# A four-layer graph network on one core: 0/1 matrices on GpSimd and results kept in PSUM late in layer 0, own products earlier in the attention layer

## What is computed

```python
edge_index = jnp.stack([src, dst])                     # 25000 edges, sorted by dst
x = _layernorm(x + _L0_gnn_ref(x, Wq, Wk, Wv, src, dst))
x = _layernorm(x + _L1_gnn_ref(x, edge_index, ...))
x = _layernorm(x + _L2_gnn_ref(x, edge_index, ...))
x = _layernorm(x + _L3_gnn_ref(x, edge_index, edge_attr, ...))

# layer 0: attention without a maximum; 8 heads of 32
score = jnp.exp(jnp.clip(sum(k[src] * q[dst]) / sqrt(32), -5.0, 5.0))
out = segment_sum(v[src] * score, dst) / (segment_sum(score, dst) + 1e-09)

# layer 2: graph attention with a loop at every node
e = leaky(a_src[src] + a_dst[dst])                     # loops included
alpha = softmax of e over the edges of one dst
y = segment_sum(h[src] * alpha, dst) + bias + x
return layernorm(y) * ln_w + ln_b
```

## Time and profile before

| | |
|---|---|
| median of 3 runs | 4683.01 us (4680.12 to 4685.71) |
| profiled execution | 4724.27 us |
| its span | 4722.6 us, mean granted clock 0.948 |
| busy share of the span | PE 93%, DVE 84%, POOL 66%, ACT 56% |
| `layer0` | about 30 to 1052 us |
| `nodes1` | about 1052 to 2466 us |
| `nodes2` | about 2466 to 3490 us |
| `layer3` | about 3490 to 4722 us |

### The profile page before, as it was taken

The page is one execution under the profiler, slowest core; times in us unless marked ns, Lnnn a source line. Parts: engine busy times, 40 slices in busy tenths (PEclk is TensorE's granted clock), DMA queues, the critical chain, the costliest instruction groups (busy, mean ns, idle before and its releaser), DMA issues. The chain is left out here.

```text
span 4722.6 us, 90136 instructions
## 1 busy us (share of the span) xinstructions
PE 4413.9 (93%) x21114; PEld 3442.3 (73%) x21114; DVE 3984.7 (84%) x12084; ACT 2635.3 (56%) x6042; POOL 3105.5 (66%) x3736
## 2 busy tenths in 40 slices
PE   6999998769999999999987999999969999999998
PEld 4666664438888888888866777777746666688887
DVE  4677778988999999999974888988867777888887
ACT  2787886544555555555553777777741111255554
POOL 4555552227777777777746888888746666588887
PEclk8999997559999999999997999999989999999999
DMA  5977777983444444444445899999855555788885
GB/s 156 244 219 223 222 219 247 296 251 106 153 152 152 148 149 152 152 152 147 150 155 161 274 275 274 277 274 274 259 158 175 175 175 175 228 260 261 263 261 173
DMA packets 911651, 970.50 MB, mean 206 GB/s; under 512 B 104938, under 2 KB 867672, under 8 KB 911306
## 3 DMA queue, kind: packets, MB, share of 16 engines
q1 hardware_dynamic: 501268, 472.10, 34.2%
q10 hardware_dynamic: 327254, 315.21, 19.6%
q0 software_dynamic: 82784, 179.41, 13.2%
HBM read 654.95 MB, written 363.57 MB: 216 GB/s over the span
## 5 line engine op out<-in xcount | busy, mean ns | idle before, releaser
L601 POOL DMA_INDIRECT layer_xg<-in_x,edge_rows x392 | 387.2, 988 | 332.7 <-PE layer_t_ps L647 240.8
L936 POOL DMA_INDIRECT nodes_near_rows<-x_d,nodes_cur x392 | 418.1, 1067 | 238.1 <-POOL nodes_cur L931 169.8
L1669 POOL DMA_INDIRECT layer_xg<-x_d,edge_rows x392 | 377.6, 963 | 211.3 <-PE layer_x_ps L1742 139.5
L1244 POOL DMA_INDIRECT nodes_near_rows<-hh_d,source_row x392 | 396.0, 1010 | 128.2 <-issue 84.7
L1059 PE MATMUL nodes_h_ps<-w_h,nodes_x2T 128*128 128x272 f32 x1568 | 392.2, 393 | 8.1 <-ACT nodes_x2T L1136 8.1
L1817 ACT ACTIVATE layer_xT<-layer_x_ps 128x512 f32<-128x512 f32 x196 | 117.0, 597 | 495.5 <-PE layer_x_ps L1742 446.2
L680 PE MATMUL layer_agg<-layer_msg,layer_hot 128*128 128x264 f32 x784 | 313.1, 539 | 65.8 <-issue 65.8
L1069 PE MATMUL nodes_hid_ps<-nodes_zT,w_a 128*128 128x256 f32 x1568 | 372.3, 380 | 0.7 <-ACT nodes_zT L1143 0.7
L662 PE MATMUL layer_kv_ps<-w_kv,layer_xT 128*128 128x512 f32 x784 | 371.2, 596 | 0.9 <-DVE layer_made L806 0.9
L1049 PE MATMUL nodes_out_ps<-w_b,nodes_hid 128*128 128x256 f32 x1568 | 371.1, 380 | 0.6 <-ACT nodes_hid L1128 0.5
L1757 PE MATMUL layer_kv_ps<-w_kv,layer_xT 128*128 128x512 f32 x784 | 370.4, 595 | 0.0
(11 more groups left out here) (241 smaller groups left out, 12724.1 us busy)
## 6 DMA issues: line engine op xcount, KB each, us to landing
layer_msg<-msg_d SPq DMA_DIRECT2D x784, 132.0 KB, 3.3
nodes_xin<-x_d SPq DMA_DIRECT2D x392, 256.0 KB
hh_d<-nodes_hh ACTq DMA_DIRECT2D x196, 264.0 KB
x_d<-layer_y ACTq DMA_DIRECT2D x196, 256.0 KB
x_d<-nodes_x2b ACTq DMA_DIRECT2D x196, 256.0 KB
nodes_hin<-hh_d SPq DMA_DIRECT2D x196, 256.0 KB
x_d<-nodes_x ACTq DMA_DIRECT2D x196, 256.0 KB
layer_xin<-x_d SPq DMA_DIRECT2D x196, 256.0 KB
```

Of the source, the lines that this page charges most:

```text
L601: gp.indirect_dma_start(out=xg[:, c % 8, k, :], out_offset=None, in_=x, in_offset=bass.IndirectOffsetOnAxis(ap=edge_rows[:, c, k:k + 1], a ...
L936: gp.indirect_dma_start(out=near_rows[:, r, h, :], out_offset=None, in_=x1_d, in_offset=bass.IndirectOffsetOnAxis(ap=cur[:, r, h:h + 1], a ...
L1244: gp.indirect_dma_start(out=near_rows[:, u % NR, h, :], out_offset=None, in_=hh_d, in_offset=bass.IndirectOffsetOnAxis(ap=source_row[:, 2 ...
L1669: gp.indirect_dma_start(out=xg[:, c % 8, k, :], out_offset=None, in_=x3_d, in_offset=bass.IndirectOffsetOnAxis(ap=edge_rows[:, c, k:k + 1] ...
```

## The change

In `layer0`, for units 104 to 195: the 0/1 matrices are made by GpSimd (two `tensor_scalar`), each pair behind the unit's load of x and a wait for the sums of four units before; the division writes back into `agg`, and the addition reads it from there, so TensorE waits for `filled` of unit u-2 rather than `divided`; the moments are written to `t_ps` and read from it. For all units: the inversion of the norm moves behind the sum plus 1e-9. In `nodes2`: own products of units that are not the first of a group are issued directly behind the transposes into `work_ps`; ScalarE's copy to `own_first` moves ahead of its copies out of `work_ps`.

```diff
-    def norm_merge(ve, t, u, spare):
+    def norm_merge(ve, t, u, spare, moments=None):
+        moments = t["moments"][:, ring(u, 4), :, :] if moments is None else moments
...
+        def late_moments(u):
+            return t_ps[:, u % 4 * 4:u % 4 * 4 + 4].rearrange("p (h w) -> p h w", w=2) if u >= LATE else None
...
                 for u in range(LATE, UNITS):
                     load_x(gp, u)
+                    gp.wait_ge(summed, u - 3)
+                    for h in range(2):
+                        last = gp.tensor_scalar(hot[:, u % 4, h, :], iota[:, :], target_rel[:, 2 * u + h:2 * u + h + 1], None, ALU.is_equal)
+                    last.then_inc(late_hot, 1)
...
-                            pe.wait_ge(hot_ready, u + 1)
-                            if u >= 2:
+                            if u < LATE:
+                                pe.wait_ge(hot_ready, u + 1)
+                            else:
+                                pe.wait_ge(late_hot, u - LATE + 1)
+                            if u >= LATE + 2:
+                                pe.wait_ge(ln["filled"], u - 1)
+                            elif u >= 2:
                                 pe.wait_ge(divided, u - 1)
...
-                            u = at(U0 + 4)
-                            if u is not None:
-                                norm_invert(ve, ln, (None, 8, u))
                             u = at(U0 + 2)
                             if u is not None:
                                 ve.wait_ge(summed, u + 1)
                                 nc.vector.tensor_scalar(den[:, u % 2, :, :], agg[u % 2][:, :, D:D + H], 1e-9, None, ALU.add)\
                                     .then_inc(eps_added, 1)
+                            u = at(U0 + 4)
+                            if u is not None:
+                                norm_invert(ve, ln, (None, 8, u))
                             u = at(U0)
-                            if u is not None:
+                            if u is not None and u < LATE:
...
-                                nc.vector.tensor_tensor(by_head(mean_msg[:, u % 2, :, :]), by_head(agg[u % 2][:, :, 0:D]),
+                                to = mean_msg[:, u % 2, :, :] if u < LATE else agg[u % 2][:, :, 0:D]
+                                nc.vector.tensor_tensor(by_head(to), by_head(agg[u % 2][:, :, 0:D]),
                                                         over_head(den[:, u % 2, :, :]), ALU.mult).then_inc(divided, 1)
...
+                                if u == LATE:
+                                    ve.wait_ge(copied, EC)
+                                norm_merge(ve, ln, (None, 8, u), spare_ve, late_moments(u))
...
-                                nc.vector.tensor_tensor(ln["rows"][:, u % 4, :, :], mean_msg[:, u % 2, :, :], xin[:, u % 8, :, :], ALU.add)\
+                                mean = mean_msg[:, u % 2, :, :] if u < LATE else agg[u % 2][:, :, 0:D]
+                                nc.vector.tensor_tensor(ln["rows"][:, u % 4, :, :], mean, xin[:, u % 8, :, :], ALU.add)\
                                     .then_inc(ln["filled"], 1)
...
+                def own_product(u):
+                    pe.wait_ge(first_copied, u // GU + 1)
+                    if u >= 1:
+                        pe.wait_ge(own_done, u)
+                    for h in range(2):
+                        w = (2 * u + h) % (2 * GU)
+                        last = nc.tensor.matmul(own_ps[:, w * H:(w + 1) * H], hot[:, u % HOT, h, :],
+                                                head_columns(own_first[:, u // GU % 2, :], of_group(u // GU))[:, w, :],
+                                                start=True, stop=True)
+                    last.then_inc(own_summed, 1)
...
                         last.then_inc(both_turned, 1)
+                    u = at(15)
+                    if u is not None and u % GU:
+                        own_product(u)
                     u = at(18)
...
                     u = at(15)
-                    if u is not None:
-                        pe.wait_ge(first_copied, u // GU + 1)
...
+                    if u is not None and u % GU == 0:
+                        own_product(u)
...
                         last.then_inc(outer_normed, 1)
+                    g = at(15)
+                    if g is not None and g % GU == 0:
+                        g //= GU
+                        n = of_group(g) * H
+                        act.wait_ge(share_turned, g + 1)
+                        if g >= 2:
+                            act.wait_ge(own_summed, GU * (g - 1))
+                        nc.scalar.activation(own_first[:, g % 2, 0:n], own_ps[:, P:P + n], ACT.Copy, scale=-1.0 / BIG).then_inc(first_copied, 1)
                     u, e, k = at(2), at(2 + LATER), s - 2
```

More of the change, by code:

```diff
@@ L460, in norm_measure, with norm_root @@
         last.then_inc(t["measured"], 1)
-    def norm_merge(ve, t, u, spare):
+    def norm_merge(ve, t, u, spare, moments=None):
+        moments = t["moments"][:, ring(u, 4), :, :] if moments is None else moments
         gate(ve, spare, t["measured"], num(u) + 1)
         for h in range(2):
-            last = nc.vector.bn_aggr(t["moments"][:, ring(u, 4), h, :], t["parts"][:, ring(u, 4), h, :])
+            last = nc.vector.bn_aggr(moments[:, h, :], t["parts"][:, ring(u, 4), h, :])
         last.then_inc(t["merged"], 1)
-    def norm_root(act, t, u):
+    def norm_root(act, t, u, moments=None):
+        moments = t["moments"][:, ring(u, 4), :, :] if moments is None else moments
         act.wait_ge(t["merged"], num(u) + 1)
-        nc.scalar.activation(t["dev"][:, ring(u, 4), :], t["moments"][:, ring(u, 4), :, 1], ACT.Sqrt,
+        nc.scalar.activation(t["dev"][:, ring(u, 4), :], moments[:, :, 1], ACT.Sqrt,
                              bias=eps_ln[:, :]).then_inc(t["rooted"], 1)
@@ L475, in norm_invert, with norm_shift @@
         nc.vector.reciprocal(t["rstd"][:, ring(u, 4), :], t["dev"][:, ring(u, 4), :]).then_inc(t["inverted"], 1)
-    def norm_shift(ve, t, u):
+    def norm_shift(ve, t, u, moments=None):
+        moments = t["moments"][:, ring(u, 4), :, :] if moments is None else moments
         ve.wait_ge(t["inverted"], num(u) + 1)
-        nc.vector.scalar_tensor_tensor(t["shift"][:, ring(u, 4), :], t["moments"][:, ring(u, 4), :, 0], -1.0,
+        nc.vector.scalar_tensor_tensor(t["shift"][:, ring(u, 4), :], moments[:, :, 0], -1.0,
                                        t["rstd"][:, ring(u, 4), :], ALU.mult, ALU.mult).then_inc(t["shifted"], 1)
@@ L565, in layer0 @@
         x = a["x"]
-        first_in = sem("first_in")
+        first_in, late_hot = sem("first_in"), sem("late_hot")
         out_rows = by_chunk(msg0_d)
@@ L733, in body @@
                             if u is not None:
-                                norm_root(act, ln, (None, 8, u))
+                                norm_root(act, ln, (None, 8, u), late_moments(u))
                 run_units(UNITS, U0 + 5, body)
@@ L847, in body @@
                             if u is not None:
-                                norm_merge(ve, ln, (None, 8, u), spare_ve)
+                                if u == LATE:
+                                    ve.wait_ge(copied, EC)
+                                norm_merge(ve, ln, (None, 8, u), spare_ve, late_moments(u))
                         c = chunk_at(s, j)(2)
@@ L856, in body @@
                             if u is not None:
-                                norm_shift(ve, ln, (None, 8, u))
+                                norm_shift(ve, ln, (None, 8, u), late_moments(u))
                         else:
@@ L1580, in body @@
                         nc.scalar.activation(score_ps[0:n, 0:2 * P], score_ps[0:n, 0:2 * P], ACT.Exp).then_inc(exped, 1)
[L1581 to L1588, removed]
                     if at(19) is not None or at(22) is not None:
```

## The result

Median of 16 runs: 4693.73 us after the change, 4684.55 before; ratio 1.002, 95% interval 1.0012 to 1.0028. The kernel is 9 us slower. Forecast were 4702 us and +19.

What follows compares the result with a forecast made beforehand. VectorE, with DMA nearly full, was taken to bound late layer 0, the `work_ps` loop `nodes2`. Layer 0's -15 and `nodes2`'s +34 us gave +19 on 4724.27, 4743.3, times 0.9913: 4702 us, range 4674 to 4732.

Steps and rivals of the forecast that it cites:

- What bounds the kernel: Late layer 0: VectorE, with DMA engines nearly full beside it; `nodes2`: the loop through `work_ps`, with a 0.55 us gap.
- what is late next is the DMA: 2.51 us at a full share: Late layer 0: once VectorE is relieved, DMA limits a unit to 2.51 us, 2.53 at a share of 0.99.
- -15: Layer 0, 92 late units: each goes from 2.69 to 2.53 us; bounds 0 and -29 us, the latter at VectorE's 2.37.
- Rival (a): Layer 0: DMA has more to give, -29 us; kernel faster if `nodes2` loses under 20, 4664 us; chance 0.17.
- The bounds for PSUM: Late layer 0: division and moments in PSUM instead of SBUF cost nothing, bounds +-0.05 us a unit.
- GpSimd's queue: Late layer 0: two comparisons and one DMA issue take 1.95 us a unit, below 2.37; later loads of x cost nothing.
- Rival (d): Layer 0: GpSimd's matrices come late, a unit stays at 2.69 us, 0 instead of -15, 4717 us; chance 0.08.
- step with the first own product: `nodes2`, once a group: 5.07 us instead of 6.22, -1.15, if ScalarE has done its normalisations by then.
- the 0.16: `nodes2`, step before the score products: an early own product loses only its 0.16 us overlap with the products' tail.
- The clock: `nodes2`: no fall of TensorE's clock after the change, since the long stop at a group's first own product is gone.
- Rival (c): `nodes2`: gaps make the clock fall once a group, 24 x 1.4 = 34 us more, 4735 us; chance 0.12.
- The copy's place: `nodes2`: the early `own_first` copy delays ScalarE's queued work 0.6 us once a group, already counted in the 5.07 us step.

Runs made afterwards that it cites:

- e5: The changed kernel without 157 of 171 early own products, from the third group on; run once, ordinary `nodes2` step 4.39 us against 4.83.
- e9: The changed kernel with half the aggregation moved behind the products for `e` in `nodes2`: ratio to before 0.9821, 4599.4 us against 4682.3.
- e10: e1 without the norm's statistics of layer 0's units from 108 on; run once, a unit takes about 2.13 us, at up to 381 GB/s.
- e8: The kernel before with only layer 0's late division and moments in PSUM, 0/1 matrices still on VectorE: ratio to before 1.0000.
- e2: `nodes2` of the changed kernel, layer 0 of the kernel before: ratio to before 1.0084, +40 us.
- e3: e1 with ScalarE's copy to `own_first` moved ahead, own products all at their old place: ratio to before 0.9895, 22 us less than e1.
- e4: e3 with half the aggregation moved behind the products for `e`: ratio to before 0.9907, 6 us more than e3.
- e1: Layer 0 of the changed kernel, `nodes2` of the kernel before: ratio to before 0.9942, 4699.8 us against 4726.9.

## Why the prediction was right, and where it was not

**What bounds the kernel: right in `nodes2`, half right in layer 0.** The loop over `work_ps` was read as it is: e5 shows that the early product adds its length to the ordinary step, and e9 that the step shrinks as soon as other work fills the gap of 0.55 us. In layer 0 VectorE was the bound, and my reading that the DMA engines were nearly full was wrong.

**Layer 0: mechanism right, size wrong.** VectorE's own 2.37 us were worked out and 2.38 measured. The step that failed is "what is late next is the DMA: 2.51 us at a full share". I took bytes per share at 99% as the rate of a full engine. The runs moved 338 GB/s at 2.38 us and 381 in e10. The share counts the time of packets, and the bytes per us of share are no constant: from before to e10 SP's reads went from 0.303 to 0.345 MB/us of share (6.57/(0.381 x 50)), GpSimd's from 0.301 to 0.387 (6.30/(0.326 x 50)), while ScalarE's writes stayed at 0.35. So -15 should have been my own lower bound, -29; measured -27. Rival (a) was right in its mechanism but not in its sign, which it tied to a loss in `nodes2` of under 20 us. The Trainium skill (DMA: Bandwidth & Descriptors, Specifications) gives some 358 GB/s as HBM's limit for a core. By it layer 0 would have got the right term, and the 338 GB/s of after lie under it; but it is no limit in this case, since the 381 of e10 lie above it.

**The bounds for PSUM: right.** From 850 to 950 us the division takes 670 ns and the addition 656 before, 676 and 667 in e8: 0.02 us a unit, inside the +-0.05, and e8's time shows no change. After the change they are 681 and 674.

**GpSimd's queue: right.** 2 x 0.61 + 0.76 = 1.97 us a unit (1.95 forecast), and VectorE never waited for x. Rival (d), the unit staying at 2.69, did not come about.

**`nodes2`, step by step.** Forecast and measured, in us: ordinary step 4.88, 4.83; step behind the score products 4.83, 4.77; step before them 5.25, 5.09; step with the first own product 5.07, 4.92; step behind it 5.27, 5.43. Sum 39.96 and 39.53. An own product is worth 0.45, not 0.50. Before the score products even the 0.16 was not lost: the product was never free there. Against the 38.14 of a group without a fall of the clock that is +1.39 instead of +1.82.

**The clock: the term that was wrong.** I let the falls vanish with the long stop. They came more often and cost more: 10 of 22 groups at 1.68 us (7.11 - 5.43), 0.76 a group in the mean. Before, it was 7 of the 22 groups that have a second step with transposes, not of 24, so 1.39 x 7/22 = 0.44 and a mean of 38.58 instead of 38.55. That makes 40.29 - 38.58 = +1.71 a group, x 24.5 = +42 by the profile and +40 in e2, against +34. Rival (c) had the direction and a half of its size.

**The sum: close in part by luck.** Its terms were further off than the sum. In layer 0 the forecast was 12 us too high. In `nodes2` the steps were 0.43 us a group too high (39.96 against 39.53, some 10 us) and the falls of the clock, at nothing, some 19 us too low. Forecast were +19 and measured +9; the parts measured alone add up to +13, which the intervals allow.

**The copy's place: right, and underrated.** It went into the 5.07. Alone it is worth 22 us (e3), the only gain in this change outside layer 0, and the early products used up more than that.

## What to carry to other kernels

An operation in the gap of a loop through one buffer is free there, and it can cost nearly its full length elsewhere in the loop; before moving it, name what will stand in the gap. The early own products come with shorter waits of ScalarE for VectorE (62.9 us in e4, 27.2 in e9), and with other work in the gap both gains are kept: the change lost 40 us in this stage, the same change with half an aggregation in the gap gained some 56 (83 less layer 0's 27). A DMA share near 1 was no limit on the rate here; look at which engine has no idle time, and take the cost of a byte at that share as an upper bound only.

## What the runs showed of the hardware

From 900 to 950 us the share of the DMA engines was 0.97 before and 1.06 in e10, while the rate went from 300 to 381 GB/s. In e10 a packet is 0.94 KB in SP's queue, 0.96 in ScalarE's and 3.3 in GpSimd's.

TensorE's clock, by rows. Late in layer 0 it stood at 1.2 GHz throughout with stops of 0.59 us in 2.69. After the change the mean of the window is 0.74 of full speed: sometimes the four matmuls take 1.13 us with stops of 1.25, sometimes 2.10 with stops of 0.27 (e1), at the same 2.37 us a unit. In `nodes2` a stop of 0.56 us in every 4.83 did not lower it. Two stops of 0.37 and 0.39 us within 1.5 us, right behind such steps, lowered it in 10 of 22 groups (11 of 22 in e2). The same two stops in e9, where the ordinary steps have no stop, lowered it in none of 22. A single one of 1.03 in e3 never did, and one of 1.58 before in 7 of 22. So the stops before the pair matter too; what decides between the groups of one run was not tried.
